# Placing the first batch's query and key rows between the natural scores instead of ahead of them, in a post-norm decoder layer

## The reference

```python
qkv = x @ w_qkv + b_qkv
att = einsum('bhqd,bhkd->bhqk', q, k) * scale
att = softmax(where(causal, att, -inf))
y = einsum('bhqk,bhkd->bhqd', att, v)
x = layernorm(x + y @ w_proj + b_proj)
```

## Time and profile before

| | |
|---|---|
| median of three runs | 652.57 us (649.79, 652.57, 653.44) |
| the profiled execution's own time | 653.15 us |
| its span, first to last instruction | 651.4 us |
| PE busy, share of the span | 619.9 us, 95% |
| DVE busy | 491.0 us, 75% |
| ACT busy | 326.6 us, 50% |
| POOL busy | 229.1 us, 35% |

### The profile page before, as it was taken

One profiled execution on the slowest core, in us unless ns is written; L12 is line 12 of the kernel. 1 busy time (PEld: TensorE's weight loads), 2 busy tenths in 40 slices (PEclk: granted clock), 3 DMA queues, 4 the chain that ended last, 5 costly groups with the idle time before them and its releaser, 6 DMA issues.

```text
span 651.4 us, 13981 instructions
## 1 busy us (share of the span) xinstructions
PE 619.9 (95%) x5064; PEld 564.7 (87%) x5080; DVE 491.0 (75%) x1037; ACT 326.6 (50%) x734; POOL 229.1 (35%) x276
## 2 busy tenths in 40 slices
PE   8989999999989899999999999999999997999996
PEld 7767777787779899999999999999999986999995
DVE  4565677677746888979888798887998988667653
ACT  5434555555764456573555745566465644131220
POOL 9603435243453431332313323133222115161542
PEclk9799999999999999999999999999999999899999
DMA  9545567365200400000000000000000000132250
GB/s 314 156 131 173 154 190 210 108 202 175 62 18 1 162 2 2 17 18 1 0 0 16 16 0 0 0 0 0 0 2 2 1 1 1 51 115 85 81 162 33
DMA packets 31710, 43.34 MB, mean 67 GB/s; under 512 B 3408, under 2 KB 19248, under 8 KB 31664
## 3 DMA queue, kind: packets, MB, share of 16 engines
q1 hardware_dynamic: 31392, 42.47, 20.9%
q10 hardware_dynamic: 272, 0.26, 0.1%
HBM read 29.39 MB, written 13.21 MB: 65 GB/s over the span
## 4 chain that ended last, share of the span: by engine, by line
PE 65%; DVE 14%; issue 13%; POOL 4%; ACT 3%; another core or an unknown queue 0%; DVEq 0%; POOLq 0%; ACTq 0%
PE bank L449 28%; PE bank L2172 11%; PE bank L1984 4%; PE bank L1884 3%; POOL hid_hl L797 3%; PE bank L1842 2%; PE bank L1849 2%; PE bank L1865 2%; PE bank L457 2%; PE bank L2001 2%; PE bank L1970 1%; PE bank L1869 1%; PE bank L1851 1%; DVE attn L1380 1%; PE bank L1993 1%
## 5 line engine op out<-in xcount | busy, mean ns | idle before, releaser
L449 PE MATMUL bank<-slots_hl,whhT_hl 128*128 128x256 f32 x864 | 113.2, 284 | 0.0
L449 PEld LDWEIGHTS bank<-slots_hl,whhT_hl 128*128 128x128 f32 x864 | 105.7, 188 | 2.4 <-ACT gate_z L1101 1.0
L2172 PE MATMUL bank<-attn_hl,vg_hl 128*128 128x256 f32 x864 | 105.5, 280 | 0.2
L2172 PEld LDWEIGHTS bank<-attn_hl,vg_hl 128*128 128x128 f32 x864 | 100.7, 188 | 4.4 <-ACT attn_hl L811 3.9
L1290 DVE TENSOR_REDUCE neg_max<-bank 128x2 f32<-128x512 f32 (+1 forms) x96 | 65.5, 690 | 42.1 <-PE bank L1851 28.5
L867 ACT ACTIVATE pT<-bank 128x512 f32<-128x512 f32 x96 | 56.9, 598 | 44.5 <-PE bank L1865 29.0
L688 POOL TENSOR_TENSOR sq<-sq 128x256 f32<-128x256 f32 x24 | 18.1, 754 | 170.5 <-ACT sq L1086 130.2
L674 POOL TENSOR_SCALAR_AFFINE_SELECT pT<-pT 128x512 f32<-128x512 f32 x64 | 40.4, 636 | 100.6 <-ACT pT L867 100.6
L449 PE MATMUL bank<-values_hl,hid_hl 128*128 128x256 f32 x384 | 49.4, 287 | 0.3 <-DVE x L1560 0.3
L797 POOL TENSOR_TENSOR hid_hl<-hid,hid_hl 128x512 fp32r<-128x512 f32 x32 | 40.9, 1303 | 24.7 <-ACT hid_hl L811 24.6
L449 PE MATMUL bank<-x2T_hl,keys_hl 128*128 128x256 f32 x384 | 48.6, 284 | 0.0
(11 more groups left out here) (216 smaller groups left out, 1300.6 us busy)
## 6 DMA issues: line engine op xcount, KB each, us to landing
gate_rows<-gate_mem SPq DMA_DIRECT2D x48, 128.0 KB, 3.0
q_rows<-q_hl SPq DMA_DIRECT2D x21, 256.0 KB, 2.8
k_rows<-k_hl SPq DMA_DIRECT2D x21, 256.0 KB, 2.6
q_op<-q_rows SPq DMA_DIRECT2D x28, 192.0 KB, 3.2
k_op<-k_rows SPq DMA_DIRECT2D x14, 384.0 KB, 4.4
x_in<-in_x_dram SPq DMA_DIRECT2D x8, 256.0 KB, 3.1
c_in<-in_ctx_dram SPq DMA_DIRECT2D x8, 256.0 KB, 2.8
out_dram<-y_out SPq DMA_DIRECT2D x8, 256.0 KB, 2.7
```

What stands on the lines that cost most here:

```text
L449: mm = pe.matmul(dst, left(a), right(b), start=first and n == 0, stop=last and n == 2, skip_group_check=True)
L2172: mm = pe.matmul(halves(b)[:, m, :], vg_hl[:, j, v_part, 3 * t + r, q:q + P], attn_hl[:, j, at_part, t, :], start=n == 2 and a + m + t == ...
```

## The change

`set_rows(1)` to `set_rows(3)` leave the place ahead of the loop on PE; each stands now within the loop, right behind `natural(quad, 0)` of the group before it: `natural(0, 0)`, `set_rows(1)`, `natural(0, 1)`, `natural(0, 2)`, `natural(1, 0)`, `set_rows(2)` and so on. DVE's `set_keys(1)` to `set_keys(3)` go the same way behind the first reduction of a group. ACT's list keeps its order: `set_queries(1)` to `set_queries(3)` stay ahead of the three weight copies. The values of the first two batches (`v` 0, `v` 1), which stood both behind `natural(0, 0)`, stand behind `natural(0, 2)` and `natural(1, 2)`; PE's waits for the low parts of weights and keys and for POOL's fills of constants (`consts` at 19) now stand behind `natural(0, 2)`. Four small steps of DVE on biases move from ahead of the loop to (quad, third) = (4, 1), and ACT no longer waits for them at quad 0. In DVE's loop the items of `FIRST_BESIDE` are read behind the keyed work of the same third instead of ahead of it: at (0, 2) this turns round `context_weights_lo(1)` and `keys_lo(3)`.

```diff
-        FIRST_BESIDE = {(-4, 0): [("v", 0), ("v", 1)], (-1, 2): [("w", 0)], (0, 2): [("w", 1)], (1, 0): [("w", 2)],
+        FIRST_BESIDE = {(-4, 2): [("v", 0)], (-3, 2): [("v", 1)], (-1, 2): [("w", 0)], (0, 2): [("w", 1)], (1, 0): [("w", 2)],
                         (1, 2): [("w", 3)], (2, 2): [("w", 4)]}
...
-        W_READ = (10, 11, 12, 13, 14)
+        W_READ = (6, 7, 8, 9, 10)
...
                     act.wait_ge(prep_mm, 1)
-                    act.wait_ge(prep_dve, 8)
                     act.wait_ge(prep_pool, 3)
...
             first_operand_lo(1, k_hl, bq_col[:, NC:2 * NC], k_hi, k_lo, 7)
-            for s in range(1, 4):
-                set_keys(s)
-            step(dve.tensor_tensor(brz_col[:, :], bih_col[:, 0:4], bhh_col[:, 0:4], ALU.add))
-            step(dve.tensor_scalar(brz_col[:, :], brz_col[:, :], 0.5, None, ALU.mult))
-            step(dve.tensor_scalar(bhh_col[:, 2 * NC:], bhh_col[:, 2 * NC:], 0.5, None, ALU.mult))
-
-            step(dve.tensor_scalar(slot_col[:, :], slot_col[:, :], float(D) ** -0.5, None, ALU.mult))
-            dve.wait_ge(w_in[4], 16)
-            dve.wait_ge(consts, 19)
...
                     if quad + LEAD < QUADS:
                         maxima(quad + LEAD, third)
-                    for name, n in FIRST_BESIDE.get((quad, third), ()):
-                        if name == "v":
-                            values_out(n, BESIDE_BANK["v", n, 0])
-                        else:
-                            context_weights_lo(n)
+                    if third == 0 and quad + LEAD < 3:
+                        set_keys(quad + LEAD + 1)
+                    if (quad, third) == (-LEAD, 2):
+                        dve.wait_ge(w_in[4], 16)
+                        dve.wait_ge(consts, 19)
...
                     elif key == (7, 2) and 0 <= 2 * period < B:
                         residual(2 * period)
+                    for name, n in FIRST_BESIDE.get((quad, third), ()):
+                        if name == "v":
+                            values_out(n, BESIDE_BANK["v", n, 0])
+                        else:
+                            context_weights_lo(n)
+                    if (quad, third) == (4, 1):
+                        step(dve.tensor_tensor(brz_col[:, :], bih_col[:, 0:4], bhh_col[:, 0:4], ALU.add))
+                        step(dve.tensor_scalar(brz_col[:, :], brz_col[:, :], 0.5, None, ALU.mult))
+                        step(dve.tensor_scalar(bhh_col[:, 2 * NC:], bhh_col[:, 2 * NC:], 0.5, None, ALU.mult))
+
+                        step(dve.tensor_scalar(slot_col[:, :], slot_col[:, :], float(D) ** -0.5, None, ALU.mult))
...
             project_first(7, 1, 1)
-            for s in range(1, 4):
-                set_rows(s)
-            pe.wait_ge(prep_dve, 4)
-
-            pe.wait_ge(k_lo, 2)
-            pe.wait_ge(consts, 19)
             for quad in QUADS_AND_TAIL:
                 for third in range(3):
                     if quad + LEAD < QUADS:
                         natural(quad + LEAD, third)
+                    if third == 0 and quad + LEAD < 3:
+                        set_rows(quad + LEAD + 1)
+                    if (quad, third) == (-LEAD, 2):
+                        pe.wait_ge(prep_dve, 4)
+
+                        pe.wait_ge(k_lo, 2)
+                        pe.wait_ge(consts, 19)
                     if 0 <= quad < QUADS:
                         turned(quad, third)
```

## The result

The changed kernel takes 656.49 us (median of 18 runs, 654.97 to 659.34), the kernel before 652.56 (18 runs): a ratio of 1.0061, with a 95% interval of 1.0047 to 1.0075, or +3.9 us. In a second comparison, of 12 runs, the ratio was 1.0043 (1.0022 to 1.0063). The profiled execution of the changed kernel took 655.88, its span is 654.2. Two executions far above all others, one of 747 us in experiment 1 and one of 1844 us of the kernel before beside it, are left out of the ratios.

What follows compares the result with a forecast made beforehand. PE's list, in its order, was taken to set the time. +1.8 (later `q` 2) + 1.1 (slow clock) - 1.5 (`w` 2) = +1.4 on the profiled 653.15: 654.6, or 654.0 against the median; range 651.0 to 658.0.

Steps and rivals of the forecast that it cites:

- rival 2: Clock falls already among the placements, and again in the stand before `q` 2: +4.0, 656.6 us; chance 0.20.
- The new path of PE: PE from first placement to second pair of `set_rows(3)`: 10.8 us at full clock, from 14.7 to 25.5.
- The new wait: Before `q` 2, PE stands 5.9 us for the text behind ACT's and POOL's 5.8 us chain; `q` 2 starts 1.8 later.
- The gain at `w` 2: At (0, 2), `k` 3's low part made earlier removes PE's 1.50 us wait before `w` 2: -1.5.
- The clock after the stand: From `q` 2, products run slowly for 3.4 us, as after the fall at 553.8: +1.1, bounds 0 and 2.3.
- the first (a full clock): PE stands before `q` 2 but the clock stays full: +0.3, 652.9 us; chance 0.13.
- The third (no stand): Text ready when PE comes, `q` 2 starting at 26.3 instead of 30.38: -5.6, 647.0 us; chance 0.10.

Runs made afterwards that it cites:

- experiment 1: Changed kernel with the second text's high parts ahead of ACT's last query copy and low parts ahead of POOL's projection-weight low part: 648.53 us, ratio 0.9949.
- experiment 4: Changed kernel with only ACT's list edited (second text's high parts ahead of the last query copy), POOL's list as it was: 654.69 us, ratio 1.0043.
- experiment 2: Kernel before with only DVE's order turned round, low part of `k` 3 ahead of that of `w` 1: 650.13 us, ratio 0.9973.
- experiment 5: Changed kernel run again as it is, against the kernel before: 655.30 us, ratio 1.0043.
- experiment 3: Changed kernel with 24 needless products on PE while it waits for the text before `q` 2: 653.49 us, ratio 1.0029.
- experiment 8: Kernel of experiment 1 with the second half of the text's low part moved from POOL to DVE: 649.11 us, ratio 0.9936.
- the shared version: Kernel of experiment 1 with the text's low part shared between POOL and DVE, run twice: 649.11 us (ratio 0.9936) and 647.30 us (0.9929).
- experiment 6: Kernel before with only `v` 0 and `v` 1 moved between the placements, natural scores left behind them: 654.68 us, ratio 1.0032.

## Why the prediction was right, and where its size was off

The forecast was +1.4, 654.0 us, in a range of 651.0 to 658.0; measured was 656.49. This is above the forecast's own part of the range (652.5 to 656) and is the number of rival 2 (656.6), whose mechanism did not occur. The mechanism of the forecast did, with one term mis-sized.

- **The new path of PE** held: 25.5 was expected for the second pair of `set_rows(3)`, and ACT starts to copy it near 25.2 in a run that is 0.45 ahead. The full clock among the placements, which I took over rival 2, held too: the values ran at 1.68.
- **The new wait** held in place, cause and size: 5.9 us expected, 5.76 measured, by the chain of ACT and POOL (5.8 expected, 5.7 measured). `q` 2 came 1.7 later, 1.8 expected. Experiments 1 and 4 show that it is this chain, and that POOL's link is needed for it; the two edits of experiment 1 were not parted any further.
- **The gain at `w` 2** held: -1.5 expected, -1.67 in the profile, -1.8 in the median of experiment 2 (between -0.3 and -3.2).
- **The clock after the stand** is the term that was mis-sized. I put its price at 1.1, "the row in which PE was busy after standing", with bounds of 0 and 2.3. In the profile it was 3.70 from `q` 2 to `w` 0, above the upper bound (1.58 in that of experiment 5, within it). The length was wrong: the low level lasted 9.0 us of work in this profile and 4.1 in that of experiment 5, not 3.4. The rate was wrong as well, by a reading of the earlier trace rows: 3.7 of 9.0 is 0.41, not a third. The 0.142 divides the whole duration of a line by its products, with the slow start of the first and the end of the last in it, and of the 5.11 behind the 0.213 the last 0.8 ran at the full clock. PE's timeline of the kernel before has products of the same shape from within both lines:

```profile
13.29 1.23 PE L2061 MATMUL bank<-xT_hl,wqkv_hl 128*128 128x256 f32 x9
```

```profile
21.64 2.76 PE L449 MATMUL bank<-wqkv_hl,xT_hl 128*128 128x256 f32 x12
```

A single one lasts 0.28 in the first and 0.42 in the second, so they start (1.23 - 0.28) / 8 = 0.119 and (2.76 - 0.42) / 11 = 0.213 apart. The `128x512` products start 0.231 apart in the kernel before's `q` 2 and 0.427 in the changed kernel's. So 44 to 46% of the low time is lost with either shape: for 3.4 us that would have been 1.5, and 3.0 for the upper bound. The Trainium skill's rule (TensorE: Matmul & The Clock Gate, Back-to-back issue gap), nearly twice the spacing, agrees with the trace (1.79 and 1.85 times); the prediction was wrong to set it aside.
- With 3.7 for 1.1 the sum would have been +1.4 + 2.6 = +4.0, where the medians show +3.9; with the 1.6 of experiment 5 it would have been +1.9, where they show +2.6. So the agreement to a tenth in the first is partly luck.
- Of the **rivals**, the first (a full clock) is what experiment 3 made by force. The second (a fall among the placements) did not occur, though its number came out: the clock was full until 27.0. The third (no stand) is nearly what experiments 1 and 8 made: -5.6 was forecast for it; -3.4 and -3.1 were measured in the two runs with a stand of 1 us, -3.6 and -5.6 in those of the shared version. So the new order was worth that much once the text was in time, and the order of two other engines' lists turned it into a loss.

## What to carry to other kernels

When work moves later on one engine, look at each engine that reads its result and ask what stands behind that read in its own list; here three weight copies and a subtraction without haste stood between the last placement and the text that PE wanted next, and reordering and sharing the work turned a loss of 2.6 to 3.9 us into a gain of 3.6 to 5.6. A stand of PE can cost more than its length: here 4.1 or 9.0 us of work behind it ran at the low clock, and lost 1.6 or 3.7. Price such products by the distance from start to start, not by a line's duration over its count. An interleaving has to be judged as a mixture: in the execution profiled, the heavy products alone between the placements only moved the slow stretch.

## What had not been expected of the hardware

- The low clock is not a matter of standing alone. It fell after 3.2 us of unbroken 32-row placements in the kernel before. It fell at 26.98 in experiment 6, after naturals with 1.3 us of waits. In experiment 1 it fell at the end of a stand of 1.06 us behind placements, where the 1.50 us before `w` 2, among larger products, left the clock full in the kernel before. Yet the stand before `q` 2 matters: with one of 1.04 us or more the clock fell in it, or within 0.7 us behind it, in all six profiled executions of the new order, with one of 0.38 or less in none of three (experiment 3, and the shared version twice).
- The same program does not meet the same clock in each execution. In the three sessions of experiments, the kernel before had a mean granted clock of 0.995 in 8 of 77 executions, with a mean time of 649.6 us, 0.993 in 21 (651.3), and 0.990 in 16 (653.3); the profiled one had 0.991. So one profile shows one such outcome. The profile of before that I counted from holds 6.8 us at the low clock from the placements on, so part of what the new order gains against it may be missing against an execution with a fuller clock. This goes with experiment 3, whose median is 1.5 over the kernel before and whose profile is 0.2 over it, but it was not shown directly, and what sets the moment of a fall stays open.
